# Layers' attention: V projected in full 128-token tiles and laid out by DMA, exps and normed output in single buffers

## The chip, the core and the metric

The kernel runs on one core of a Trainium2 chip. The metric is device time in microseconds, from the start of the program to its end; lower is better. TensorE is called PE below, VectorE DVE, ScalarE ACT, GpSimd POOL, and SyncE, which issues the DMAs, SP.

## What is computed

Sixteen sequences of 256 tokens with 128 channels go through four blocks, each followed by a layer norm. The change lies in the last block, six layers of local attention and a gated feed-forward. Of its reference this matters here:

```python
def attn_layer(x, Wqkv, qs, ksc, Wo):
    qkv = x @ Wqkv                       # x: 256 x 128, Wqkv: 128 x 3072
    q, k, v = split into 16 heads of 64
    q, k = l2norm(q) * qs, l2norm(k) * ksc, both rotated by position
    out = local_attention(q, k, v)       # windows of 32 queries
    return out @ Wo

def local_attention(q, k, v):            # w = 32, nw = 8 windows
    # window i sees the 64 keys and values of windows i-1 and i
    sim = einsum('bhwie,bhwje->bhwij', bq, bk2) * 8; masked
    attn = softmax(sim)
    return einsum('bhwij,bhwje->bhwie', attn, bv2)

for i in range(6):
    x = attn_layer(shift_tokens(x), ...) + x
    x = ffn_layer(shift_tokens(x), ...) + x
```

Everything is float32, except the mask, which is added to the scores as a bfloat16 matmul.

## The kernel before

`l1_network` holds the six layers. The order of work is written out by hand for each engine, in functions of the same name that run in the same order; semaphores join them (`after(engine, semaphore, value)` waits). A layer is a `prologue` (the first sequence's projections), then 16 times `attention(N, u, ...)`, in pairs u = 0, 1: the first pair stands alone, a loop makes passes for pairs 1 to 6, the last pair stands alone again. The feed-forward follows. `attention` has two half steps, j = 0 and 1, one for each 128 tokens of sequence N, and in both it also makes half of the projections of sequence N + 1 and finishes the output of the half before.

PE's order in a half step: wait for the turned weights (`weights_ready`), `masks`, `weigh` of the half before, two `project_qk` of the next sequence, two `project_v` of the next sequence, `scores`, `output`, two `turn_output`, `turn_weights`, then four `turn_qk` and two `project_qk` among each other. Four banks of PSUM, `pp`, are shared: q and k use banks 0 and 1, everything else alternates between 2 and 3, and a bank is taken again once the use before last has been read. The second `turn_output` of a half step so waits for DVE's `add_attention`.

V is needed with the 64 tokens of a window of keys (two windows of 32) on the partitions where the turned weights have them. PE multiplies 64 rows at a time (`weigh`), the weights and the values of the even and odd channel blocks (f = 0, 1) lying on partitions 0 to 63 and 64 to 127. A window with odd number takes its 64 values from `V`, one with even number from `Vx`, which is `V` shifted by 32 tokens. `project_v(N, m)` makes `V` for 64 tokens (m = 0 to 3) by two matmuls, one for each f, to the lower and the upper half of the partitions (L2061 to L2067); `copy_v` (ACT, L2311) copies the bank to `V[:, u, m, :]`, and once all four are there (`s_V`), SP makes `Vx` by four DMAs of whole rows (L1914 to L1918). `weights_ready` waits for both before the first half is weighed. u is the parity of the sequence: V and Vx have two buffers each.

The weights: DVE takes the maximum of the scores (`maxima`, L2450), subtracts it into `E`, ACT takes the exp in place (`exps`), DVE sums (`sum_exps`), PE turns them (`turn_weights`) and ACT copies them (`copy_weights`). After `weigh`, DVE scales into `On` (`norm_output`, L2470), PE turns it (`turn_output`) and ACT copies it. `E` and `On` have one buffer for each j. POOL adds the rotary products and normalises q and k.

Of the kernel before, what the change touches and what calls it, by code (L numbers as in the profile page):

```python
# [13 lines left out]
ACT = mybir.ActivationFunctionType  # L14
# [1659 lines left out]
def l1_network(nc, env, weights, consts):  # L1674
# [50 lines left out]
    with ExitStack() as ctx:  # L1725
# [37 lines left out]
        qkT = sb("qkT", [P, 2, I // P, T])  # L1763
        V = sb("V", [P, 2, 4, 512])
        Vx = sb("Vx", [P, 2, 4, 512])
        E = sb("E", [P, NT, 2, 512])
# [4 lines left out]
        On = sb("On", [P, NT, 2, 512])  # L1771
# [22 lines left out]
        s_vx = [sem(f"v_shifted{u}", False) for u in range(2)]  # L1794
# [83 lines left out]
        def _(sp):  # L1878
# [6 lines left out]
            with sp.Fori(0, LAYERS) as l:  # L1885
# [24 lines left out]
                with sp.Fori(0, NB // 2) as i:  # L1910
                    for u in range(2):

                        N = l * NB + 2 * i + u
                        after(sp, s_V, 4 * N + 4)  # L1914
                        for f in range(2):
                            lo, hi = 64 * f, 64 * f + W
                            sp.dma_start(Vx[lo:lo + W, u, 1:4, :], V[hi:hi + W, u, 0:3, :]).then_inc(s_vx[u], 16)
                            sp.dma_start(Vx[hi:hi + W, u, :, :], V[lo:lo + W, u, :, :]).then_inc(s_vx[u], 16)  # L1918
# [114 lines left out]
        def _(pe):  # L2033
# [27 lines left out]
            def project_v(N, m, bank):  # L2061
                after(pe, s_xT, N + 1)
                wv = wqkv[:, 2 * I:3 * I].rearrange("p (c f n) -> p f c n", c=4, f=2)
                for f in range(2):
                    last = nc.tensor.matmul(pp[64 * f:64 * f + 64, bank, :].rearrange("p (c n) -> p c n", c=4),  # L2065
                                            xT[:, 64 * m:64 * m + 64], wv[:, f, :, :], start=True, stop=True)
                last.then_inc(s_v, 1)  # L2067
# [9 lines left out]
            def turn_output(N, k, bank):  # L2077
                j, f = k // 2, k % 2
                after(pe, s_On, 4 * N + k + 1)
                for c in range(4):  # L2080
                    last = nc.tensor.transpose(pp[:, bank, c * P:(c + 1) * P], On[:, j, f, c * P:(c + 1) * P],  # L2081
# [33 lines left out]
            def turn_weights(N, j):  # L2115
                for e in range(2):
                    after(pe, s_On, 4 * N + 2 * j)
                    after(pe, s_E, 4 * N + 2 * j + e + 1)
                    for c in range(4):
                        last = nc.tensor.transpose(pW[:, e, c * P:(c + 1) * P], E[:, j, e, c * P:(c + 1) * P],  # L2120
# [18 lines left out]
            def weights_ready(pair, N, u, j):  # L2139
                after(pe, s_ET, 4 * N + 2 * j + 2)  # L2140
                if j == 0:
                    after(pe, s_V, 4 * N + 4)
                    pe.wait_ge(s_vx[u], 64 * (pair + 1))
# [151 lines left out]
        def _(act):  # L2295
# [15 lines left out]
            def copy_v(N, u, m, bank):  # L2311
                after(act, s_PV, 4 * (N - 1))
                after(act, s_v, 4 * N + m + 1)
                nc.scalar.copy(V[:, u, m, :], pp[:, bank, :]).then_inc(s_V, 1)
# [14 lines left out]
            def exps(N, j, e):  # L2329
                after(act, s_sub, 4 * N + 2 * j + e + 1)  # L2330
                nc.scalar.activation(E[:, j, e, :], E[:, j, e, :], ACT.Exp).then_inc(s_E, 1)  # L2331
# [394 lines left out]
```

## Time and profile before

| | us |
|---|---|
| median of 3 runs | 5327.94 (5325.83 to 5335.15) |
| profiled execution | 5325.95 |
| its span, first to last instruction | 5324.1 |
| mean granted TensorE clock | 0.933 of full |

| engine | busy us | share |
|---|---|---|
| PE matmul | 4457.0 | 84% |
| PE weight loads (beside the matmuls) | 3018.6 | 57% |
| DVE | 3369.7 | 63% |
| POOL | 2571.8 | 48% |
| ACT | 2441.2 | 46% |

The six layers take from about 1255 us to the end, the 96 sequences of attention most of that. A matmul of 512 columns in float32 shows as two records. In the timelines neighbouring records of one line are merged, so that a merged row's length runs to the modelled end of the last; the starts are exact. "issue" as the cause of an idle time means that the engine waited for nothing that the profile shows. Line numbers are those of the kernel before.

### The profile page before, as it was taken

Reading aid. Unit: us, or ns where it says so; the run is one execution under the profiler, and the core shown is the slowest. Engines: PE = TensorE matmul, PEld = TensorE weight load, DVE = VectorE, ACT = ScalarE, POOL = GpSimd, SP = SyncE. Lnnn points to the kernel's source line nnn. Section 1 sums busy time; section 2 is a strip of 40 time slices with the busy share of each in tenths; the row PEclk is TensorE's granted clock in tenths of the full one; section 3 lists DMA queues with packets and bytes.
Section 4 is the critical chain, followed back from the end, with each engine's and each line's share of the span. In section 5 each row is a group of like instructions: output and inputs, shape, how many; then the busy total and the mean of one; then the engine's idle time right before and its main releaser. Section 6 shows DMA issues by size and latency. Waiting matters only on the chain. (4 is left out here: it accounts for less than half of the span.)

```text
span 5324.1 us, 183366 instructions
## 1 busy us (share of the span) xinstructions
PE 4457.0 (84%) x70226; PEld 3018.6 (57%) x70227; DVE 3369.7 (63%) x7024; ACT 2441.2 (46%) x5161; POOL 2571.8 (48%) x4541
## 2 busy tenths in 40 slices
PE   8999938676888888888888888888888888888885
PEld 5777725563555555555555555555555556555563
DVE  3555532475766567766677666766667666676765
ACT  4555543133554435554355544544435554354542
POOL 0000000004776547775376753767537776377761
PEclk9999959797999999999999999999999999999997
DMA  1000003101111101111011110111101111011110
GB/s 37 4 4 4 1 0 80 30 0 54 31 30 24 39 20 31 30 24 39 20 31 24 30 40 20 31 24 30 40 20 25 29 30 33 20 31 30 30 23 32
DMA packets 76046, 143.02 MB, mean 27 GB/s; under 512 B 19654, under 2 KB 57748, under 8 KB 68116
## 3 DMA queue, kind: packets, MB, share of 16 engines
q1 hardware_dynamic: 75284, 131.92, 10.3%
q8 instruction: 593, 9.72, 0.8%
q14 instruction: 169, 1.38, 0.1%
HBM read 35.40 MB, written 4.19 MB: 7 GB/s over the span
## 5 line engine op out<-in xcount | busy, mean ns | idle before, releaser
L2439 DVE TENSOR_TENSOR n_tt<-n_pp,n_rot 128x1024 f32<-128x1024 f32 x768 | 925.3, 1222 | 650.8 <-ACT n_sq L2309 647.8
L1941 POOL TENSOR_TENSOR n_pre<-n_tt 128x512 f32<-128x512 f32 x768 | 965.6, 1276 | 481.5 <-DVE n_tt L2439 480.8
L2057 PE MATMUL n_pp<-n_wqkv,n_xT 128*128 128x512 f32 x1536 | 828.6, 643 | 10.6 <-ACT n_xT L2304 10.5
L2309 ACT ACTIVATE n_sq<-n_pp 128x512 f32<-128x512 f32 x768 | 458.9, 598 | 797.2 <-PE n_pp L2057 793.4
L1976 POOL TENSOR_TENSOR n_pre<-n_pre,n_rn 128x512 f32<-128x512 f32 x768 | 777.6, 1045 | 36.8 <-POOL n_rn L1964 36.8
L2446 DVE TENSOR_REDUCE n_ss<-n_sq 128x8 f32<-128x512 f32 x768 | 519.5, 676 | 0.0
L2331 ACT ACTIVATE n_E<-n_E 128x512 f32<-128x512 f32 x384 | 235.8, 630 | 595.6 <-DVE n_E L2458 595.6
L2074 PE MATMUL n_pp<-ident,n_pre 128*128 128x128 f32 x3072 | 416.0, 278 | 45.4 <-POOL n_pre L1976 41.8
L2074 PEld LDWEIGHTS n_pp<-ident,n_pre 128*128 128x128 f32 x3072 | 361.3, 144 | 161.5 <-issue 94.4
L2320 ACT COPY n_qkT<-n_pp 128x512 f32<-128x512 f32 x768 | 420.7, 604 | 54.3 <-PE n_pp L2074 52.8
L2088 PE MATMUL n_pp<-n_wo,n_OT 128*128 128x128 f32 x3072 | 406.4, 287 | 4.9 <-ACT n_OT L2326 4.9
L2476 DVE TENSOR_TENSOR n_On<-n_pW,n_ri 128x512 f32<-128x512 f32 x384 | 246.8, 685 | 225.9 <-PE n_pW L2133 224.9
L2088 PEld LDWEIGHTS n_pp<-n_wo,n_OT 128*128 128x128 f32 x3072 | 369.8, 197 | 23.6 <-ACT n_OT L2326 6.2
L2081 PE MATMUL n_pp<-ident,n_On 128*128 128x128 f32 x1536 | 241.8, 281 | 165.8 <-DVE X L2483 165.2
L2065 PE MATMUL n_pp<-n_wqkv,n_xT 128*64 128x512 f32 x1536 | 379.2, 612 | 0.0
L2133 PE MATMUL n_pW<-n_V,n_ET 64*32 64x64 f32 x12288 | 325.2, 237 | 39.9 <-issue 39.7
L2108 PEld LDWEIGHTS n_pS<-n_qkT 64*32 64x32 f32 x24576 | 254.2, 105 | 173.2 <-issue 173.2
L2057 PEld LDWEIGHTS n_pp<-n_wqkv,n_xT 128*128 128x128 f32 x1536 | 260.8, 201 | 158.0 <-issue 135.4
L2133 PE MATMUL n_pW<-n_Vx,n_ET 64*32 64x64 f32 x12288 | 309.4, 236 | 47.2 <-issue 41.4
L2453 DVE TENSOR_REDUCE n_nm<-n_pS 128x8 f32<-128x512 f32 x384 | 247.4, 686 | 139.8 <-PE n_pS L2108 139.8
L556 DVE CUSTOM_DVE_ANT_0 a_S<-a_pS,a_causal 128x128 f32<-128x128 f32 (+1 forms) x512 | 162.7, 356 | 264.9 <-PE a_pS L361 211.5
L296 POOL TENSOR_TENSOR a_rstd<-a_mv,neghalf 128x2 f32<-128x2 f32 x16 | 11.2, 701 | 653.1 <-DVE a_mv L124 653.1
(263 smaller groups left out, 8241.4 us busy)
## 6 DMA issues: line engine op xcount, KB each, us to landing
n_Vx<-n_V SPq DMA_DIRECT2D x192, 256.0 KB, 3.8
n_Vx<-n_V SPq DMA_DIRECT2D x192, 192.0 KB, 3.7
n_wqkv<-in_L_ffn_Wqkv SPq DMA_DIRECT2D x6, 1536.0 KB, 7.4
e_w<-in_L_ffn_w SPq DMA_DIRECT2D x32, 256.0 KB, 3.0
m_Y<-e_ye SPq DMA_DIRECT2D x64, 64.0 KB, 2.0
n_wo<-in_L_ffn_Wo SPq DMA_DIRECT2D x6, 512.0 KB, 7.2
a_xs<-in_L_attn_x SPq DMA_DIRECT2D x16, 128.0 KB, 2.1
x_kept<-X SPq DMA_DIRECT2D x1, 2048.0 KB, 8.5
```

The source lines that it names most:

```text
L1941: nc.gpsimd.tensor_tensor(d, s[0], s[1][:, :, ::-1, :], ALU.add).then_inc(s_add, 1)
L1976: nc.gpsimd.tensor_tensor(d, d, bcast(rn[:, j, t, 8 * half:8 * half + 8], 2, D), ALU.mult).then_inc(s_kn, 1)
L2057: nc.tensor.matmul(pp[:, c % 2, :], xT[:, j * P:(j + 1) * P], wqkv[:, t * I + 512 * half:t * I + 512 * half + 512], start=True, stop=True) ...
L2065: last = nc.tensor.matmul(pp[64 * f:64 * f + 64, bank, :].rearrange("p (c n) -> p c n", c=4), xT[:, 64 * m:64 * m + 64], wv[:, f, :, :], s ...
L2074: last = nc.tensor.transpose(pp[:, bank, g * P:(g + 1) * P], pre[:, j, t, o:o + P], ident[:, :])
L2088: last = nc.tensor.matmul(pp[:, bank, 0:C], OT[:, j, k % 2, k // 2, :], wo[:, k, :], start=(k == 0), stop=(k == I // P - 1))
L2108: last = nc.tensor.matmul(pS[W * w:W * w + W, e, i * 2 * W + o:(i + 1) * 2 * W], qkT[r:r + D, 0, i, q:q + W], qkT[r:r + D, 1, i, lo:q + W] ...
L2133: last = nc.tensor.matmul(pW[W * w:W * w + W, f, o:o + D], ET[r:r + D, e, c, W * w:W * w + W], v[r:r + D, u, m, o:o + D], start=True, stop ...
L2309: nc.scalar.activation(sq[:, c % 2, :], pp[:, c % 2, :], ACT.Square).then_inc(s_sq, 1)
L2320: nc.scalar.copy(qkT[:, t, 4 * half:4 * half + 4, j * P:(j + 1) * P], pp[:, bank, :].rearrange("p (g q) -> p g q", g=4)).then_inc(s_qkT, 1)
L2439: nc.vector.tensor_tensor(tt[:, c % 4, :, :].rearrange("p s (h d) -> p s h d", d=D), bcast(pp[:, c % 2, :].rearrange("p (h d) -> p h d", d ...
L2446: nc.vector.tensor_reduce(ss[:, j, t, 8 * half:8 * half + 8], sq[:, c % 2, :].rearrange("p (h d) -> p h d", d=D), AX.X, ALU.add).then_inc( ...
```

## The change

`project_v(N, m)` now makes one matmul of 128 tokens by 512 of V's 1024 channels (m counts half of the tokens and half of the channels). ACT copies it to a plain buffer `Vn` (token on the partition, two groups of 128 tokens, one buffer for all sequences). SP makes both layouts from it, 18 DMAs to a sequence instead of 4: after the first half's two copies ten, after the second's eight. Each of them takes 32 or 64 tokens and for each token four runs of 128 channels (512 bytes), which are side by side at the destination. `s_vx` counts all of them (18 x 16 = 288 a sequence). PE waits for `s_vx` alone before it weighs. ACT, before each copy to `Vn`, waits until the sequence before has been placed; it needs the pair's number for that. `E` and `On` lose their dimension j, and their writers wait for the reader of the half step before instead of that of the sequence before.

```diff
         nt = sb("nt", [P, 2 * H])
         pre = sb("pre", [P, NT, 2, I])
         qkT = sb("qkT", [P, 2, I // P, T])
+        Vn = sb("Vn", [P, NT, I])
         V = sb("V", [P, 2, 4, 512])
         Vx = sb("Vx", [P, 2, 4, 512])
-        E = sb("E", [P, NT, 2, 512])
+        E = sb("E", [P, 2, 512])
         ET = sb("ET", [P, 2, 4, P])
         nm = sb("nm", [P, NT, 2, 8])
         rs = sb("rs", [P, NT, 2, 8])
         ri = sb("ri", [P, NT, 2, 8])
-        On = sb("On", [P, NT, 2, 512])
+        On = sb("On", [P, 2, 512])
         OT = sb("OT", [P, NT, 2, 4, P])
...
-        s_vx = [sem(f"v_shifted{u}", False) for u in range(2)]
+        s_vx = [sem(f"v_placed{u}") for u in range(2)]
...
                         N = l * NB + 2 * i + u
-                        after(sp, s_V, 4 * N + 4)
-                        for f in range(2):
-                            lo, hi = 64 * f, 64 * f + W
-                            sp.dma_start(Vx[lo:lo + W, u, 1:4, :], V[hi:hi + W, u, 0:3, :]).then_inc(s_vx[u], 16)
-                            sp.dma_start(Vx[hi:hi + W, u, :, :], V[lo:lo + W, u, :, :]).then_inc(s_vx[u], 16)
+                        for j in range(NT):
+                            after(sp, s_V, 4 * N + 2 * j + 2)
+                            for f in range(2):
+                                lo, hi = 64 * f, 64 * f + W
+                                own = Vn[:, j, :].rearrange("p (c f n) -> p f c n", c=4, f=2)[:, f, :, :]
+
+                                def place_v(to, rows, m, src):
+                                    sp.dma_start(to[rows:rows + src.shape[0], u, m, :].rearrange(
+                                        "p (c n) -> p c n", c=4), src).then_inc(s_vx[u], 16)
+
+                                place_v(V, lo, 2 * j, own[0:64, :, :])
+                                place_v(V, lo, 2 * j + 1, own[64:P, :, :])
+                                place_v(Vx, hi, 2 * j, own[0:W, :, :])
+                                place_v(Vx, lo, 2 * j + 1, own[W:P - W, :, :])
+                                if j == 0:
+                                    place_v(Vx, lo, 2, own[P - W:P, :, :])
...
             def project_v(N, m, bank):
                 after(pe, s_xT, N + 1)
-                wv = wqkv[:, 2 * I:3 * I].rearrange("p (c f n) -> p f c n", c=4, f=2)
-                for f in range(2):
-                    last = nc.tensor.matmul(pp[64 * f:64 * f + 64, bank, :].rearrange("p (c n) -> p c n", c=4),
-                                            xT[:, 64 * m:64 * m + 64], wv[:, f, :, :], start=True, stop=True)
-                last.then_inc(s_v, 1)
+                j, half = m // 2, m % 2
+                nc.tensor.matmul(pp[:, bank, :], xT[:, j * P:(j + 1) * P],
+                                 wqkv[:, 2 * I + 512 * half:2 * I + 512 * half + 512],
+                                 start=True, stop=True).then_inc(s_v, 1)
...
             def weights_ready(pair, N, u, j):
                 after(pe, s_ET, 4 * N + 2 * j + 2)
                 if j == 0:
-                    after(pe, s_V, 4 * N + 4)
-                    pe.wait_ge(s_vx[u], 64 * (pair + 1))
+                    after(pe, s_vx[u], 288 * (pair + 1))
...
-            def copy_v(N, u, m, bank):
+            def copy_v(N, u, m, bank, pair):
                 after(act, s_PV, 4 * (N - 1))
+                after(act, s_vx[1 - u], 288 * (pair + u))
                 after(act, s_v, 4 * N + m + 1)
-                nc.scalar.copy(V[:, u, m, :], pp[:, bank, :]).then_inc(s_V, 1)
+                nc.scalar.copy(Vn[:, m // 2, 512 * (m % 2):512 * (m % 2) + 512], pp[:, bank, :]).then_inc(s_V, 1)
...
-                        copy_v(N + 1, 1 - u, 2 * j, bank("v", 2 * j, 1))
-                        copy_v(N + 1, 1 - u, 2 * j + 1, bank("v", 2 * j + 1, 1))
+                        copy_v(N + 1, 1 - u, 2 * j, bank("v", 2 * j, 1), pairs[0] + u)
+                        copy_v(N + 1, 1 - u, 2 * j + 1, bank("v", 2 * j + 1, 1), pairs[0] + u)
...
-            layers(act, attention, feed_forward, prologue)
+            pairs = [None]
+
+            def on_pair(i):
+                pairs[0] = i
+
+            layers(act, attention, feed_forward, prologue, on_pair=on_pair)
...
-                after(dve, s_ETp, 4 * (N - 1) + 2 * j + 2)
+                after(dve, s_ETp, 4 * N + 2 * j)
                 for e in range(2):
                     after(dve, s_max, 4 * N + 2 * j + e + 1)
-                    nc.vector.tensor_tensor(E[:, j, e, :].rearrange("p (i s) -> p i s", s=2 * W),
+                    nc.vector.tensor_tensor(E[:, e, :].rearrange("p (i s) -> p i s", s=2 * W),
...
             def norm_output(N, j):
                 after(dve, s_ri, 2 * N + j + 1)
-                after(dve, s_OTp, 4 * (N - 1) + 2 * j + 2)
+                after(dve, s_OTp, 4 * N + 2 * j)
                 after(dve, s_PV, 4 * N + 2 * j + 2)
                 r = ri[:, j, :, :].rearrange("p e (c f) -> p f c e", f=2)
                 for f in range(2):
-                    nc.vector.tensor_tensor(On[:, j, f, :].rearrange("p (c e d) -> p c e d", c=4, e=2),
+                    nc.vector.tensor_tensor(On[:, f, :].rearrange("p (c e d) -> p c e d", c=4, e=2),
```

The other lines of the diff only drop the index j of `E` and `On` where they are read (L2081, L2120, L2331, L2465).

## Rows read from the trace of the kernel before

**Rows 1.** The page: busy time of the engines; the group of V's projection.
```profile
PE 4457.0 (84%) x70226; PEld 3018.6 (57%) x70227; DVE 3369.7 (63%) x7024; ACT 2441.2 (46%) x5161; POOL 2571.8 (48%) x4541
...
L2065 PE MATMUL n_pp<-n_wqkv,n_xT 128*64 128x512 f32 x1536 | 379.2, 612 | 0.0
```

**Rows 2.** Busy time by stretch (PE, PEld, DVE, ACT, POOL; granted clock; DMA): two sequences.
```profile
1403.75:1443.13 39.38, 32.34 (x667) 21.07 (x655) 25.18 (x37) 18.18 (x34) 25.61 (x47) 0.91 0.12 27
1443.13:1475.53 32.40, 29.53 (x668) 20.01 (x655) 24.91 (x37) 18.18 (x34) 25.17 (x45) 1.00 0.14 31
```

**Rows 3.** Timeline (start, length, engine, line, tile, count, idle), PE, one undisturbed sequence.
```profile
1447.28 0.66 PE L2081 MATMUL n_pp<-ident,n_On 128*128 128x128 f32 x4 [0.97 <-DVE X L2483]
1447.77 1.04 PE L2120 MATMUL n_pW<-ident,n_E 128*128 128x128 f32 x8
...
1454.89 1.97 PE L2057 MATMUL n_pp<-n_wqkv,n_xT 128*128 128x512 f32 x4
1456.79 1.94 PE L2065 MATMUL n_pp<-n_wqkv,n_xT 128*64 128x512 f32 x8
1458.66 1.46 PE L2108 MATMUL n_pS<-n_qkT 64*32 64x32 f32 x128
```

**Rows 4.** Timeline, PE, narrow windows that split its records around that V projection.
```profile
1456.27 0.59 PE L2057 MATMUL n_pp<-n_wqkv,n_xT 128*128 128x512 f32 x1
...
1457.70 1.03 PE L2065 MATMUL n_pp<-n_wqkv,n_xT 128*64 128x512 f32 x4
...
1458.13 0.60 PE L2065 MATMUL n_pp<-n_wqkv,n_xT 128*64 128x512 f32 x2
```

**Rows 5.** Timeline, DVE, the same sequence.
```profile
1455.50 1.28 DVE L2476 TENSOR_TENSOR n_On<-n_pW,n_ri 128x512 f32<-128x512 f32 x2
...
1460.18 1.29 DVE L2453 TENSOR_REDUCE n_nm<-n_pS 128x8 f32<-128x512 f32 x2 [0.55 <-PE n_pS L2108]
```

**Rows 6.** Timeline, ACT, copies of V in three half steps.
```profile
1403.14 0.59 ACT L2314 COPY n_V<-n_pp 128x512 f32<-128x512 f32 x1 [0.27 <-PE n_pp L2065]
...
1442.52 0.59 ACT L2314 COPY n_V<-n_pp 128x512 f32<-128x512 f32 x1 [0.27 <-PE n_pp L2065]
...
1457.92 0.59 ACT L2314 COPY n_V<-n_pp 128x512 f32<-128x512 f32 x1 [0.42 <-PE n_pp L2065]
```

**Rows 7.** Timeline, PE, the prologue of layer 1.
```profile
1936.38 1.08 PE L2065 MATMUL n_pp<-n_wqkv,n_xT 128*64 128x512 f32 x4
...
1938.45 1.08 PE L2065 MATMUL n_pp<-n_wqkv,n_xT 128*64 128x512 f32 x4
```

**Rows 8.** DMA issues (KB each, us to landing), and line 1021 (ns min/median/max).
```profile
n_Vx<-n_V SPq DMA_DIRECT2D x192, 256.0 KB, 3.8
...
m_Y<-e_ye SPq DMA_DIRECT2D x64, 64.0 KB, 2.0
...
L1021 SPq DMA_DIRECT2D m_Y<-e_ye x64: 606/608/789, 863.5 to 966.7; - x64
```

**Rows 9.** Busy time by stretch: line 1021's transfers, then V's.
```profile
948.00:950.00 2.00, 2.00 (x8) 1.03 (x7) 0.00 (x0) 1.83 (x4) 0.00 (x0) 1.00 0.31 66
1407.00:1409.00 2.00, 1.10 (x10) 1.10 (x11) 2.00 (x5) 1.55 (x4) 2.00 (x3) 1.00 1.04 229
```

**Rows 10.** Timeline, ACT, layer 1, V's last copy in the prologue, the next one.
```profile
1943.70 0.59 ACT L2314 COPY n_V<-n_pp 128x512 f32<-128x512 f32 x1 [0.42 <-PE n_pp L2065]
...
1961.94 0.59 ACT L2314 COPY n_V<-n_pp 128x512 f32<-128x512 f32 x1 [0.42 <-PE n_pp L2065]
```

**Rows 11.** Timeline, PE, at the end of a pass of the loop.
```profile
1416.48 0.60 PE L2096 MATMUL n_pS<-n_win,n_eye 128*128 128x512 bf16 x2 [2.76 <-issue]
```

**Rows 12.** Busy time by stretch, the same place.
```profile
1413.75:1414.00 0.25, 0.00 (x0) 0.00 (x0) 0.00 (x0) 0.24 (x1) 0.25 (x1) 1.00 0.24 66
1416.20:1418.90 2.70, 1.80 (x77) 1.16 (x78) 0.01 (x1) 0.00 (x0) 2.06 (x6) 0.67 0.03 6
1417.25:1423.50 6.25, 5.00 (x132) 2.83 (x112) 1.50 (x3) 0.60 (x1) 3.48 (x15) 0.50 0.01 3
```

More of the change, by code:

```diff
@@ L2080, in turn_output @@
                 for c in range(4):
-                    last = nc.tensor.transpose(pp[:, bank, c * P:(c + 1) * P], On[:, j, f, c * P:(c + 1) * P],
+                    last = nc.tensor.transpose(pp[:, bank, c * P:(c + 1) * P], On[:, f, c * P:(c + 1) * P],
                                                ident[:, :])
@@ L2119, in turn_weights @@
                     for c in range(4):
-                        last = nc.tensor.transpose(pW[:, e, c * P:(c + 1) * P], E[:, j, e, c * P:(c + 1) * P],
+                        last = nc.tensor.transpose(pW[:, e, c * P:(c + 1) * P], E[:, e, c * P:(c + 1) * P],
                                                    ident[:, :])
@@ L2330, in exps @@
                 after(act, s_sub, 4 * N + 2 * j + e + 1)
-                nc.scalar.activation(E[:, j, e, :], E[:, j, e, :], ACT.Exp).then_inc(s_E, 1)
+                nc.scalar.activation(E[:, e, :], E[:, e, :], ACT.Exp).then_inc(s_E, 1)
             def copy_weights(N, j, e):
@@ L2345, in prologue @@
                     elif kind == "v":
-                        copy_v(N, 0, c, bank)
+                        copy_v(N, 0, c, bank, l * (NB // 2))
                     else:
@@ L2464, in sum_exps @@
                     after(dve, s_E, 4 * N + 2 * j + e + 1)
-                    nc.vector.tensor_reduce(rs[:, j, e, :], E[:, j, e, :].rearrange("p (i s) -> p i s", s=2 * W),
+                    nc.vector.tensor_reduce(rs[:, j, e, :], E[:, e, :].rearrange("p (i s) -> p i s", s=2 * W),
                                             AX.X, ALU.add).then_inc(s_rs, 1)
```

## The prediction

> **What bounds the kernel now.** I read four views in this order: the page's busy shares, the busy time of single sequences, the timelines of TensorE (PE) and VectorE (DVE) inside one sequence, and the DMA issues. By the page PE is busy 84% of the span, the next engine 63% [rows 1]. Inside one sequence of the layers PE is busy 29.53 of 32.40 us while DVE has 24.91 and GpSimd (POOL) 25.17 [rows 2], so in this stage PE's queue sets the pace. PE does not run free: once in each half step it waits 0.97 us for DVE's addition to X before turn_output [rows 3]. That wait is the end of a chain that begins with the last score matmul: DVE's maxima, subtractions, one sum of squares, the addition. But DVE itself was idle for 0.55 us before those maxima, waiting for the scores [rows 5]. So time that PE saves ahead of the scores moves the whole chain forward, up to 0.55 us in a half step; beyond that DVE is late.
>
> The second thing to see is the end of a pass of the loop over pairs of sequences. A sequence that holds it takes 39.38 us instead of 32.40 [rows 2]: PE idles 2.76 us with nothing to wait for but its own issue [rows 11], a short transfer of 66 GB/s x 0.25 us = 16 KB lies at its start, and from 1417.25 to 1423.50 the granted clock is 0.50, that is the level of 1.2 GHz, right after that idle time [rows 12]. The loop has six passes in each of six layers, so this happens 30 times: about 30 x 7 = 210 us of the span, which the change does not aim at but could disturb.
>
> **V's projection, PE.** Before, one project_v is two matmuls on 128x64 tiles, on the two column halves of the array. They run side by side: two project_v take 1458.66 - 1456.79 = 1.87 us with 8 records [rows 3], where eight one after the other at the 0.43 us between 1457.70 and 1458.13 [rows 4] would take 3.4. The full tile has one matmul (two records) with the same 512 columns, so the streaming time stays 2 x 0.43 = 0.86 us; halving the number of matmuls gains nothing by itself. What goes is the change of tile shape between the projections of q, k and of V. The last q/k record starts at 1456.27 [rows 4] and V starts at 1456.79 [rows 3], 0.52 instead of 0.43: 0.09 us. The first two V records take 1457.70 - 1456.79 = 0.91 instead of 0.86: 0.05 us. After the last V record (1458.13) [rows 4] the scores, again another shape, start at 1458.66 [rows 3], 0.53: this 0.10 stays, because 128x128 to 64x32 is a change too. Saving per half step 0.09 + 0.05 = 0.14 us; it lies on PE's path and is below DVE's 0.55. V is projected for the next sequence in 15 of 16 steps, two half steps each, six layers: 180 x 0.14 = 25.2 us. Bounds: 0 if the 0.14 belongs to something else than the shape, 180 x 0.24 = 43 us if the exit goes as well.
>
> In the prologue V and q/k alternate: from one V to the next 1938.45 - 1936.38 = 2.07 us [rows 7] instead of 1.72, but there DVE's rotation and sum follow closely and I grant only 0.3 us to a layer: 1.8 us (0 to 6 x 1.05 = 6.3).
>
> **The copies of V, ScalarE (ACT).** Still four of 0.59 us to a sequence [rows 6], now to Vn. New is the wait on the placement of the previous sequence's V ahead of each. Behind it on ACT stand the exps, the copies of the turned output and of the weights, and PE and DVE wait for all of these, so a late placement would cost in full.
>
> **The placement, SyncE (SP) and DMA.** Before: 4 DMAs, 2 x (192 + 256) = 896 KB, with the landing of the larger at 3.8 us [rows 8]. After: 18 DMAs, ten after the first half's copies (per f three of 128 KB and two of 64 KB, together 1024 KB) and eight after the second's (896 KB), in runs of 512 bytes. The nearest rows are those of line 1021, SBUF to SBUF, 64 KB in runs of 512 bytes: 608 ns to issue (606 to 789), 2.0 us to land [rows 8]. Its transfers moved 66 GB/s at a share of 0.31, so 213 GB/s at full share, V's large ones 229 at 1.04, so 220 [rows 9]: short runs cost little. At 213 GB/s the second burst takes 4.2 us and the first 4.8; the issues take 8 x 0.61 = 4.9 and 10 x 0.61 = 6.1 us. So the second placement is down 4.9 + 3.8 = 8.7 us after the copies (6.9 with the landing of 2.0). Its deadline: the copy that ends the second half ends at 1442.52 + 0.59 = 1443.11, and the next to Vn starts at 1457.92 [rows 6], 14.8 us later. Cover left: 6 us. It is gone from (14.8 - 3.8) / 8 = 1.38 us an issue on. The first burst hasn't to be down before that either, only to leave SP's queue free after 16 us. In each layer's prologue all 18 follow one another: the last copy ends at 1943.70 + 0.59 = 1944.29, the next is at 1961.94 [rows 10], and even with nothing issued before the last copy 18 x 0.61 + 3.8 = 14.8 us fit into 17.7. V is weighed more than half a step later still. Cost: nothing. SP does nothing else inside the layer; the feed-forward weights are issued ahead of the loop as before.
>
> Against this stands a rule of the Trainium skill, DMA: Bandwidth & Descriptors, section Bandwidth: small transfers are dominated by their descriptors, 64 KB taking 0.95 us at 138 GB/s. By that figure an estimate for the second burst is 896 KB / 138 GB/s = 6.5 us instead of 4.2; it would still be down before the deadline. This case's row for 64 KB, 213 GB/s at full share, speaks for more.
>
> **E and On in one buffer each.** maxima now waits for the turned weights of the half step before: PE did those at 1447.77 to 1448.81 [rows 3], and the next maxima start at 1460.18 [rows 5], 11 us later. norm_output waits for the half before's turned output, done at 1447.94 [rows 3], and starts at 1455.50 [rows 5]. Both are long satisfied and in both cases PE's own order guarantees it. Behind those waits on DVE stand rotations and maxima, but nothing is held. Cost nothing.
>
> **PE's program is shorter.** Each project_v loses two weight loads and two matmul records; one pass of the loop is 32 instructions shorter, and what stands ahead of the loop in a layer 48 or a few more. After the idle 2.76 us PE starts masks and weigh, does 77 matmuls and 78 loads, and stops again within 1416.20 to 1418.90 with 0.9 us idle in that window [rows 12]. I read this as the end of a block of code, with the next one still to be fetched. A head that lies 50 instructions earlier in its block has 50 more to do before the stop, at this rate (155 in about 1.3 us) up to 0.4 us at each of 30 places. I take 0.1: 3 us (bounds 0 to 12).
>
> **Sum.** 25.2 + 1.8 + 3 = 30 us. Profiled execution: 5325.95 us (span 5324.1), so 5296. The median of the three runs is 5327.94, 2 us above it: 5298.
>
> **Rivals.** *No gain.* The full tile streams as the pair did and the 0.14 us is not the shape's, or it comes back at the loop's end, whose slow stretch differs from pass to pass. For it: the column halves already overlap perfectly, and the first saving is a third of a microsecond in 32. Against it: the 0.09 and 0.05 are there, while records of one shape stand 0.43 apart. 5318 to 5338; chance 0.19.
>
> *The placement is late* (slower). If an issue of 256 runs costs not 0.61 but, say, 1.6 us, because the queue takes runs and not bytes, the second placement ends 8 x 1.6 + 3.8 = 16.6 us after the copies, 1.8 past the deadline, once for each of 90 sequences: 162 us, 5460. For it: there are 1792 runs where there were 64 long ones; against it: line 1021 shows 0.61 for 128 runs. It decides from 1.38 us an issue on. Chance 0.08.
>
> *The placement meets the loop's end* (slower). At 1403.14 + 0.59 = 1403.73 [rows 6] the last copy ends, at 1413.75 PE's code is fetched [rows 12]; if the DMA engines are then still busy, the two fetches that follow each other wait behind up to 2 us of queued transfers, 30 x 4 = 120 us, 5418. It takes a burst that lasts over 10.0 us; I have 6.9 to 8.7. Chance 0.06.
>
> *The loop's head crosses a block* (slower than forecast). The first stop after the idle time comes 77 + 78 = 155 records past the head [rows 12]. If moving the head by 50 instructions puts it at the very end of a block, PE does nearly nothing before the second fetch, and the 1.3 us of those records are lost 30 times: 39 us, so 5337 (with the 3 us above not gained, 5340). It decides if the head stands less than 50 instructions into its block now, which no row here shows. Chance 0.07. The Trainium skill, Runtime: NRT & Kernel Launch, section Instruction fetch mechanics, has the rule behind it: only sequential code is fetched ahead, in blocks of 16 KB or 256 instructions, and a taken branch out of the window fetches its target first. By that rule, the trace agrees (idle with the cause "issue", and 16 KB moved), and an estimate from its 256 puts the head some 85 to 100 into its block, 35 to 50 after the change, on the safe side.
>
> **Chances and range.** Forecast (5285 to 5316) 0.55; more than forecast, with the exit of the shape too or shorter slow stretches, 0.05 (down to 5268: 43 + 6.3 + 12 = 61 us). About 0.2% (11 us) is what this measurement can tell from no change. Faster 0.60, same 0.19, slower 0.21. The range takes in the lower bound and, above, the block rival: 5268 to 5345; it leaves out the two late-transfer rivals.
>
> **What would show it.** PE: from the first q/k projection to the scores 3.63 us instead of 3.77 (1454.89 to 1458.66), undisturbed sequences 32.1 instead of 32.4. DVE's idle before maxima down by 0.14. ACT's copies of V still wait for PE only, not for a DMA; issues near 0.6 us. Wrong it is if SP's issues pass 1.4 us, if ACT's copies wait for DMA, or if the idle at the loop's end grows beyond 2.8 us.

## The result and the profile after

| | before | after |
|---|---|---|
| median of 4 runs, us | 5329.66 (5325.83 to 5335.15) | 5242.58 (5238.51 to 5245.6) |
| ratio, 95% interval | | 0.9835 (0.9818 to 0.9852) |
| span of the profiled execution, us | 5324.1 | 5236.7 |

The change makes the kernel 87 us faster; I had forecast 30, and my range ended at 60. The page of the changed kernel, first PE and the other engines, then V's projection and the two groups of weigh (with the idle time ahead of their matmuls and its cause), then the DMAs of the placement:

```profile
PE 4403.9 (84%) x69459; PEld 3064.0 (59%) x69459; DVE 3355.6 (64%) x7024; ACT 2443.9 (47%) x5161; POOL 2569.8 (49%) x4541
...
L2076 PE MATMUL n_pp<-n_wqkv,n_xT 128*128 128x512 f32 x768 | 370.6, 603 | 0.0
...
L2144 PE MATMUL n_pW<-n_V,n_ET 64*32 64x64 f32 x12288 | 310.3, 238 | 24.8 <-issue 24.8
...
L2144 PE MATMUL n_pW<-n_Vx,n_ET 64*32 64x64 f32 x12288 | 309.5, 238 | 18.0 <-issue 12.5
...
n_V<-n_Vn SPq DMA_DIRECT2D x768, 128.0 KB, 2.6
n_Vx<-n_Vn SPq DMA_DIRECT2D x384, 128.0 KB, 2.5
n_Vx<-n_Vn SPq DMA_DIRECT2D x576, 64.0 KB, 2.2
```

V's projection keeps PE busy 370.6 us instead of 379.2 [rows 1] with half the records: as predicted, the two column halves had already run side by side. The same two groups of weigh in the kernel before:

```profile
L2133 PE MATMUL n_pW<-n_V,n_ET 64*32 64x64 f32 x12288 | 325.2, 237 | 39.9 <-issue 39.7
L2133 PE MATMUL n_pW<-n_Vx,n_ET 64*32 64x64 f32 x12288 | 309.4, 236 | 47.2 <-issue 41.4 <-ACT n_ET L2336 5.7
```

The two groups alternate within weigh. Their idle time with the cause "issue", added up, fell from 81.1 to 37.3 us. Weigh isn't touched by the change at all. I had not looked at it.

The saving of the half step that I did forecast is there. The timeline of PE in the changed kernel, and of DVE beside it:

```profile
1450.31 1.99 PE L2069 MATMUL n_pp<-n_wqkv,n_xT 128*128 128x512 f32 x4
1452.13 1.88 PE L2076 MATMUL n_pp<-n_wqkv,n_xT 128*128 128x512 f32 x4
1453.94 0.29 PE L2119 MATMUL n_pS<-n_qkT 64*32 64x32 f32 x9
```
```profile
1455.47 1.29 DVE L2469 TENSOR_REDUCE n_nm<-n_pS 128x8 f32<-128x512 f32 x2 [0.40 <-PE n_pS L2119]
```

From the first q/k projection to the scores 1453.94 - 1450.31 = 3.63 us, where [rows 3] have 3.77. DVE's idle time ahead of the maxima went from 0.55 [rows 5] to 0.40. So PE's saving did pass through to DVE.

For the whole account I took the starts of PE's records in each of the 30 passes of the loop over pairs (from one branch back to the next; two sequences) and formed the mean of every step. One pass takes 71.47 us before and 68.69 after, 2.78 less, and 30 x 2.78 = 83 of the 87 us lie there.

| step of a pass, start to start, us | before | after | less |
|---|---|---|---|
| first weigh, behind the branch | 3.24 | 2.74 | 0.50 |
| q/k projections right after it | 3.27 | 2.85 | 0.42 |
| second weigh | 2.27 | 1.41 | 0.86 |
| third weigh | 1.44 | 1.41 | 0.03 |
| fourth weigh | 2.08 | 1.41 | 0.67 |
| the other three pairs of q/k projections | 5.71 | 5.46 | 0.25 |
| V's four projection pairs | 7.58 | 7.39 | 0.19 |
| everything else | 45.88 | 46.02 | -0.14 |

A weigh is 128 weight loads and 128 matmuls, and runs through in 1.41 us if nothing stops it. Counted in instructions of PE from the branch, the stops of the kernel before inside weigh stand always at the same three places: 159, 927 and 2207. These are 159, 159 + 3 x 256 and 159 + 8 x 256, so PE's code comes in blocks of 256 instructions. The page lists the packets that carry it, 593 of 16 KB each:

```profile
q8 instruction: 593, 9.72, 0.8%
```

In the changed kernel the only stop inside weigh in a pass stands at 209. Around one stop of the kernel before, in the fourth weigh of a pass, busy time by stretch (stretch, length, then PE, PEld, DVE, ACT, POOL, granted clock, DMA share and GB/s):

```profile
1467.75:1468.00 0.25, 0.25 (x2) 0.08 (x1) 0.25 (x1) 0.25 (x2) 0.25 (x1) 1.00 0.30 66
1468.90:1469.90 1.00, 1.00 (x95) 0.96 (x95) 1.00 (x2) 0.25 (x1) 1.00 (x2) 1.00 0.00 0
1470.00:1470.50 0.50, 0.03 (x2) 0.00 (x0) 0.50 (x2) 0.00 (x0) 0.50 (x2) 1.00 0.00 0
1470.50:1471.00 0.50, 0.42 (x34) 0.34 (x33) 0.50 (x1) 0.00 (x0) 0.50 (x2) 1.00 0.00 0
```

Such a packet (0.25 us x 66 GB/s = 16 KB) begins to move just before 1468; PE goes through weigh at 95 loads and 95 matmuls a microsecond, stands still from 1470.0 and goes on at 1470.5, some 2.6 us after the packet. No other transfer is under way while it waits (DMA share 0.00), so it isn't contention. The fourth weigh of a pass in the changed kernel, in full:

```profile
1463.80:1464.05 0.25, 0.25 (x3) 0.00 (x0) 0.25 (x2) 0.18 (x1) 0.25 (x1) 1.00 0.34 72
1464.20:1465.60 1.40, 1.40 (x129) 1.31 (x128) 1.40 (x2) 0.27 (x1) 1.40 (x2) 1.00 0.00 0
```

Here a packet comes at 1463.8 too, but the block in use lasts longer than weigh does. Over the stops of all passes, in these two kernels and in the variants below, PE goes on 2.1 to 3.0 us after the start of the packet, 2.5 in the mean.

### The profile page after: what moved, and what is told of

Read it like the earlier page. It is cut to its first block and busy times, and to the rows that moved or that the text cites. A ratio compares the mean times of both kernels' runs of the same rounds, so it can differ in the third digit from the quotient of the medians.

```text
span 5236.7 us, 183609 instructions
## 1 busy us (share of the span) xinstructions
PE 4403.9 (84%) x69459; PEld 3064.0 (59%) x69459; DVE 3355.6 (64%) x7024; ACT 2443.9 (47%) x5161; POOL 2569.8 (49%) x4541
## 3 DMA queue, kind: packets, MB, share of 16 engines
q8 instruction: 593, 9.72, 0.8%
## 5 line engine op out<-in xcount | busy, mean ns | idle before, releaser
L2069 PE MATMUL n_pp<-n_wqkv,n_xT 128*128 128x512 f32 x1536 | 823.2, 639 | 10.4 <-ACT n_xT L2314 10.1
L2331 ACT COPY n_qkT<-n_pp 128x512 f32<-128x512 f32 x768 | 423.7, 603 | 68.3 <-PE n_pp L2085 66.1
L2076 PE MATMUL n_pp<-n_wqkv,n_xT 128*128 128x512 f32 x768 | 370.6, 603 | 0.0
L2144 PE MATMUL n_pW<-n_V,n_ET 64*32 64x64 f32 x12288 | 310.3, 238 | 24.8 <-issue 24.8
L2144 PEld LDWEIGHTS n_pW<-n_Vx,n_ET 64*32 64x32 f32 x12288 | 265.4, 111 | 109.8 <-issue 109.8
```

Source lines behind the costliest of these rows:

```text
L2069: nc.tensor.matmul(pp[:, c % 2, :], xT[:, j * P:(j + 1) * P], wqkv[:, t * I + 512 * half:t * I + 512 * half + 512], start=True, stop=True) ...
L2076: nc.tensor.matmul(pp[:, bank, :], xT[:, j * P:(j + 1) * P], wqkv[:, 2 * I + 512 * half:2 * I + 512 * half + 512], start=True, stop=True). ...
L2144: last = nc.tensor.matmul(pW[W * w:W * w + W, f, o:o + D], ET[r:r + D, e, c, W * w:W * w + W], v[r:r + D, u, m, o:o + D], start=True, stop ...
L2331: nc.scalar.copy(qkT[:, t, 4 * half:4 * half + 4, j * P:(j + 1) * P], pp[:, bank, :].rearrange("p (g q) -> p g q", g=4)).then_inc(s_qkT, 1)
```

## The experiments

There were two theories at first. **A, code blocks**: the shape of the tile brings what was forecast, and the other 55 to 60 us come from PE's program being shorter, so that its blocks end elsewhere. **B, data movement**: short runs in place of long rows, or the single buffers, freed something. All waits added below are for a semaphore that has long had its value.

**V in two tiles again.** In the changed kernel:

```diff
-                nc.tensor.matmul(pp[:, bank, :], xT[:, j * P:(j + 1) * P], wqkv[...512 columns...],
-                                 start=True, stop=True).then_inc(s_v, 1)
+                for e in range(2):
+                    o = j * P + 64 * e
+                    last = nc.tensor.matmul(pp[64 * e:64 * e + 64, bank, :], xT[:, o:o + 64],
+                                            wqkv[...the same 512...], start=True, stop=True)
+                last.then_inc(s_v, 1)
```

> The changed kernel with V projected in two 128x64 tiles again (two matmuls to a bank, 64 tokens each; the result and everything else as in the changed kernel). Theory A (code blocks): the change gains 25 to 33 us by one tile shape in a row and some 55 us because PE's program is shorter: the ends of its 256-instruction blocks, at instruction 159 of a loop pass before and at 209 after, no longer fall into weigh. This kernel has both undone, so about 5327 (5320 to 5335), with stops inside weigh again (before: 110 weigh phases with a gap, 81 us; after: 53, 37 us). Theory B (data movement): what went beyond 30 us comes from the placement DMAs in short runs in place of long rows, or from single buffers; then about 5272.

Measured: 5329.65 us, ratio to before 1.0007 (0.9995 to 1.0019). All of the gain is gone, with the 18 DMAs, `Vn` and the single buffers still in place. Theory B falls: together the placement and the single buffers bring and cost nothing beyond the interval, 0.12% or 6 us. The block ends are back at 161 of a pass, and so is the idle time in weigh:

```profile
L2147 PE MATMUL n_pW<-n_V,n_ET 64*32 64x64 f32 x12288 | 322.1, 234 | 55.9 <-issue 55.9
L2147 PE MATMUL n_pW<-n_Vx,n_ET 64*32 64x64 f32 x12288 | 306.7, 233 | 35.3 <-issue 29.6 <-ACT n_ET L2350 5.7
```

**Two buffers for E and On again**, PE's count unchanged:

```diff
-        E = sb("E", [P, 2, 512])
+        E = sb("E", [P, NT, 2, 512])
-                after(dve, s_ETp, 4 * N + 2 * j)
+                after(dve, s_ETp, 4 * (N - 1) + 2 * j + 2)
```

(and the same for `On` and `s_OTp`.)

> The changed kernel with E and On in two buffers each again and their old waits; PE's instruction count is unchanged. Theory A: within 0.1% of the changed kernel, 5238 to 5248. Theory B, if the single buffers bring something: slower, up to 5300.

Measured: 5235.63 us, ratio 0.9836 (0.9801 to 0.9871) beside the changed kernel's 0.9835. Nothing, as expected.

**The full tile with waits in place of the saved instructions.** In `project_v` of the changed kernel, k = 4 and then k = 8:

```diff
+                for _ in range(k):
+                    pe.wait_ge(s_clear, 3)
                 nc.tensor.matmul(pp[:, bank, :], xT[:, j * P:(j + 1) * P],
```

> The changed kernel, with four extra instructions on PE ahead of each full-tile projection of V (waits for a semaphore that has long had its value), so that its instruction count is that of two tiles. Theory A: the blocks end again where they ended before the change, the shape's gain of 25 to 33 us stays, the rest is lost: about 5298 (5290 to 5306). Theory B: the count doesn't matter, 5243 to 5250 (the waits themselves are hidden under matmuls).

> The changed kernel with eight waits ahead of each full-tile projection of V. The trace of the run with four showed that two waits stand in one instruction, so that four waits had restored only half of the count (first block end of a pass at instruction 185); eight restore all of it, with the block end at 161 as in the kernel with two tiles. Code blocks: the shape's 25 to 33 us stay and the rest goes, 5290 to 5306, with the stops near instructions 929 and 2209 of a pass back. If the length of PE's code doesn't matter: 5240 to 5255 as with four waits.

Measured: 5247.67 us (0.9847, 0.9818 to 0.9877) with four and 5312.9 (0.9979, 0.9970 to 0.9989) with eight. With four the expectation of theory A failed: the trace counts 2 instructions more for each projection, not 4, since two waits go into one instruction, and the first block end was at 185. With eight it is at 161 as with two tiles, the stops at 929 and 2209 are back, and a gain of only 0.2% is left of the 1.65%. Beside the run with two tiles at the same place (1.0007) this is the shape's share: 0.28%, 15 us, with some 8 us of uncertainty either way by the two intervals, less than the 25 I expected. Inside the passes a pair of q/k projections takes 1.82 us and one of V's 1.81, against 1.91 and 1.87 with two tiles, at the same block ends: that is the 0.14.

**The kernel before, only moved.** n waits once, at the start of PE's program for the layers, where it idles for 20 us anyway:

```diff
             pe.wait_ge(s_clear, 3)
             pe.wait_ge(s_cast, 2)
+            for _ in range(n):
+                pe.wait_ge(s_clear, 3)
```

The idle time hides only the first of them. With 206 waits the first matmul of the layers comes 1 us late. With 300 and more PE isn't ready in time: an instruction that holds two of the waits takes 0.106 us, and the first matmul comes later by 7 us with 300 waits, 10 with 362 to 372, 12 with 414, 14 with 432 and 17 with 492 (each counted from the `x_kept` DMA ahead of the layers). The first row is the kernel before, the second the one with 362 waits:

```profile
1257.90 0.69 PE L2050 MATMUL n_pp<-ident,n_xs 128*128 128x128 f32 x2 [21.32 <-DMA n_qks<-in_L_ffn_k_scale]
...
1264.39 0.68 PE L2050 MATMUL n_pp<-ident,n_xs 128*128 128x128 f32 x2 [30.94 <-issue]
```

The first branch of the layers is later by nearly the same amount, so every moved kernel below carries these microseconds once, as a cost of the padding and not of its place. The times are given as measured.

With n = 206:

> The kernel before, with 206 such waits once, at the start of PE's program for the layers, where PE idles anyway; the first block inside a pass then ends at instruction 209 instead of 159, and all later ones move with it. Nothing else is touched. Theory A: 30 to 60 us faster than before (5270 to 5300), without the stops at instructions 927 and 2207 of a pass. Theory B: 5330.

Measured: 5383.18 us, ratio 1.0105 (1.0080 to 1.0130). The move was half of what I meant, since two waits go into one instruction, and put the block end at 57 of a pass instead of 209. That a change without any work in it costs 1.05%, some 56 us, speaks for theory A even so, but it wasn't what I had expected. With n = 414:

> The kernel before with 414 waits (207 instructions) once at the start of PE's program for the layers. The first try with 206 waits moved the first block end of a pass to instruction 57 and cost 56 us; this one should put it at 208, where the changed kernel has it. Code blocks: 30 to 60 us faster than before, 5265 to 5300, stops at 927 and 2207 gone. If the first try was slower for the waits themselves: slower again, by twice as much.

Measured: 5277.31 us, ratio 0.9906 (0.9889 to 0.9923), with the block end at 208. So 0.9% of the 1.65% can be had without the change, and 1.2% if the 12 us of the waits at the start are left out. Its weigh groups:

```profile
L2133 PE MATMUL n_pW<-n_V,n_ET 64*32 64x64 f32 x12288 | 308.0, 233 | 53.9 <-issue 53.7
L2133 PE MATMUL n_pW<-n_Vx,n_ET 64*32 64x64 f32 x12288 | 306.6, 233 | 5.7 <-ACT n_ET L2338 5.7
```

53.7 us of idle time are left: the pass is 34 instructions longer than the changed one, so that with the same block end at its start another one falls at 2256 into the fourth weigh, where a stop of 0.8 us stands.

**The changed kernel, only moved**, by 432 and 372 waits:

> The changed kernel with 432 waits (some 215 instructions) once at the start, so that a pass begins near the start of a block: first block end at about instruction 250. Code blocks: the stop inside the first weigh of a pass (0.8 us a pass) goes, as all of weigh lies in the block fetched for the branch; if no other block end falls badly, 10 to 40 us faster than the changed kernel, 5200 to 5232. If the place of the blocks doesn't matter: 5241.

> The changed kernel with 372 waits (some 185 instructions) once at the start: first block end at about instruction 24 of a pass, so that the branch fetches a block of which only 24 instructions are left. Code blocks: the idle time at the head of the first weigh grows by about the 1.3 us of work that now lies behind the second fetch, 30 times 39 us, and less or more by where the other ends fall: 5265 to 5310. If the place doesn't matter: 5241.

Measured: 5258.11 us (0.9869, 0.9844 to 0.9893) and 5352.06 us (1.0056, 1.0035 to 1.0078). The first of the two missed: the block end at 1530 falls 197 instructions into the third weigh and makes a new stop of 0.78 us, more than is won at the head (0.15 us in the first weigh and 0.28 in the projections behind it), and 14 us are the waits at the start.

The second is slower than the kernel before. It has the rival of the block crossing in it, but that is only a part of its 110 us over the changed kernel. Of the 90 us by which its 30 passes are longer, the first weigh takes 1.10 us a pass, 33 us: this is the crossing, to be set against my 39, and the projections right behind it get 0.40 us a pass back. Another 27 us (0.91 a pass) stand in the third weigh, where a block end falls 226 instructions in. And the stop at the branch itself is longer, by 33 us. The row of `masks`, first in the changed kernel, then here:

```profile
L2107 PE MATMUL n_pS<-n_win,n_eye 128*128 128x512 bf16 x384 | 124.3, 408 | 93.3 <-issue 87.1 <-ACT n_qkT L2331 5.6
...
L2107 PE MATMUL n_pS<-n_win,n_eye 128*128 128x512 bf16 x384 | 126.9, 415 | 126.8 <-issue 120.6 <-ACT n_qkT L2333 5.6
```

The DMA records show why. A block ends 68 instructions ahead of the branch, so that the block behind the loop is being fetched when the branch is taken, and the packet of the branch's target starts 0.6 us behind that one. The page counts 624 code packets here instead of 593. The kernel before with its block end at 57 has the same in all 30 passes (69 instructions ahead of the branch, 624 packets), and so have 6 of the 30 passes of the changed kernel at 60 below. Where two packets overlap, PE goes on 4.7 to 4.8 us after the branch, and 3.5 to 3.7 in all other passes.

**A rule, tried blind.** Behind the head of a pass, in all kernels so far, a block end stopped a weigh (by 0.6 to 1.0 us) from its instruction 189 on, and not at 156 or earlier. The four weighs of a pass begin at 8, 678, 1350 and 2018 in the kernel before and at 8, 669, 1333 and 1992 in the changed one.

> A rule read from the seven kernels so far, tried blind: PE stops inside a weigh (256 instructions) for 0.7 to 0.9 us where a block of 256 ends behind its instruction 189 or later, and doesn't where the end is at 156 or earlier. The kernel before, with 362 waits (some 180 instructions) once at the start, puts the block ends of a pass at 235, 747, 1515 and 2027, so at 227, 69, 165 and 9 of the four weighs. By the rule only the head's stop is left, the one at 2256 of the run moved to 208 is gone (0.8 us x 30 = 24 us): 5248 to 5262. The rule being wrong: 5277 or more.

> The changed kernel with 300 waits (some 149 instructions) once at the start: block ends at 60, 828, 1340 and 2108, that is 52, 159, 7 and 116 of the four weighs. By the rule no stop behind the head; at the head 52 instead of 201 instructions of weigh before the second fetch, so 0.9 to 1.0 us more there (1.6 to 1.7 us as in the run moved to 57): 30 times 27 to 30 us more than the changed kernel, 5265 to 5275. If the head doesn't matter: 5241.

> The changed kernel with 492 waits once at the start: block ends at 220, 732, 1500 and 2012, that is 212, 63, 167 and 20 of the four weighs. By the rule (no stop at 156 or earlier, a stop from 189 on) 167 is in the open stretch. No stop there: the changed kernel's time or a little less for the shorter stop at the head, 5232 to 5243. A stop: about 5255.

Measured: the kernel before with its block ends at 235 takes 5233.51 us, ratio 0.9828 (0.9802 to 0.9854), as fast as the changed kernel, although its first matmul of the layers comes 10 us late. A gain of the whole size can be had without the change. The stops of weigh behind the head are gone in all three, as the rule has it; 167 instructions into a weigh is no stop either. Weigh's idle time in the first of them:

```profile
L2133 PE MATMUL n_pW<-n_V,n_ET 64*32 64x64 f32 x12288 | 302.4, 234 | 0.0
L2133 PE MATMUL n_pW<-n_Vx,n_ET 64*32 64x64 f32 x12288 | 298.7, 234 | 32.0 <-issue 25.9 <-ACT n_ET L2338 5.7
```

The sizes were off: 5233 where I expected 5248 to 5262, and 5305.71 (0.9949, 0.9933 to 0.9965) for the changed kernel at 60 where I expected 5265 to 5275. At 60 the stop at the head is 1.75 us instead of 0.82, 28 us in 30 passes, as expected. Of the rest 7 us are the waits at the start and 9 us are more idle time at the branch (the 6 passes with two packets), and the q/k projections run 20 us longer, with more time at the lower clock. The same 3807 us from the start of the layers on in each (columns as above), first the kernel before at 235, then the changed one at 60:

```profile
1257.00:5064.00 3807.00, 3297.72 (x63443) 2190.09 (x63444) 2662.17 (x4207) 1883.14 (x3456) 2479.13 (x4387) 0.96 0.12 29
```
```profile
1257.00:5064.00 3807.00, 3248.71 (x60942) 2221.59 (x60943) 2601.39 (x4117) 1840.54 (x3372) 2419.93 (x4269) 0.94 0.23 55
```

The clock is 0.96 on average in the one and 0.94 in the other, and 63443 matmuls are done instead of 60942. (The greater DMA share of the second is the placement.)

From 1257 us to the end the granted clock stood at its level of 1.2 GHz for 333 us in the first, 517 us in the second, 439 in the kernel before and 433 in the changed one. Of that, 126, 239, 201 and 184 us lie in the 30 passes. The stop at the head is as long at 235 as in the changed kernel, so it alone doesn't set the slow time. What does is not shown. The changed kernel at 220 took 5250.73 us (0.9861, 0.9839 to 0.9882), just above what I expected without a stop, and 17 us of that are the waits at the start: its passes are as long as the changed kernel's own (68.59 and 68.69 us).

**The shape at the good place.** The changed kernel with eight waits in `project_v` and 366 at the start, against the kernel before at 235:

> The changed kernel with both: eight waits ahead of each projection of V, so that a pass has the instruction count of two tiles, and 366 waits once at the start, so that the block ends stand at 235, 747, 1515 and 2027 as in the kernel before moved to 235. Against that run only the tile's shape differs (placement and single buffers have cost nothing). 180 half steps x 0.14 = 25 us for the shape, or the 17 us by which the runs with full and with two tiles at 161 differ: 5206 to 5218. If the shape's saving is covered by something else: 5233.

Measured: 5247.86 us, ratio 0.9861 (0.9841 to 0.9881), not faster than 0.9828. Both carry the same 10 us at the start. In its passes each pair of q/k and of V projections is shorter, 1.82 and 1.81 us instead of 1.91 and 1.87, 0.15 together, as forecast. But the block with the last projections and scores of a pass is now run through so fast that the next one isn't there: the last `scores` takes 1.93 us instead of 1.43, and the pass 68.60 instead of 68.69. What the shape saves, the fetch takes back. Outside the passes the profiled execution is 13 us slower, with 272 us at the lower clock there against 207. Why is not shown; what else differs between the two, the placement and the single buffers, cost nothing at 161, and no run measures it at 235. So the shape's 0.14 us are real and local, and what they bring to the end depends on the block ends again: 15 us at 161, nothing at 235.

**The placement's cover.** Each placement DMA is followed by one or two of the same source to spare DRAM, counted by the same semaphore (the values that are waited for grow with it):

```diff
                                     sp.dma_start(to[...], src).then_inc(s_vx[u], 16)
+                                    for _ in range(k):
+                                        sp.dma_start(env["spare"][u, next(spare), ...], src).then_inc(s_vx[u], 16)
```

> The changed kernel with each placement DMA followed by another of the same source to spare memory, both counted by the semaphore that ACT and PE wait for: 36 DMAs a sequence. In the changed kernel the last copy of a sequence ends 13.8 us before the next copy into Vn starts; 16 issues of 0.65 us and 2.6 us of landing are 13.0 us, so it should just be hidden: within 0.3% of the changed kernel, 5235 to 5260. If the placement already binds (the rival), every sequence gets about 5 us longer: 5700.

> The same with two spare DMAs behind each: 54 a sequence. SP needs 54 x 0.65 = 35 us where a sequence takes 31.4, and Vn isn't free before all have landed: 35 + 2.6 + two copies of V, 38.6 us a sequence instead of 31.4 (60 of them) and 37.2 (30, at the end of a pass): 5600 to 5800, with ACT's copies of V waiting for a DMA.

Measured: 5323.96 us (0.9991, 0.9976 to 1.0006) and 6170.44 us (one run). Neither is as expected: at twice the DMAs the cover I had put at 0.8 us isn't there. The last issue of a sequence ends 12.3 us after the last copy (median), where I had counted 10.4. The waits of ACT (us, times, longest), in the run with twice and in that with three times as many:

```profile
ACT n_Vn L2329 <- DMA spare<-n_Vn: 60.4, 32, 7.8
```
```profile
ACT n_Vn L2329 <- DMA spare<-n_Vn: 942.2, 90, 18.2
```

With twice the DMAs 32 of the 90 copies that could wait do so, 60 us together; this kernel is 81 us slower than the changed one. With three times as many all 90 wait, 10.5 us each. The changed kernel itself has no such row: its copies wait for PE alone, 109.5 us in 384 times. So the deadline that I gave exists, and the changed kernel stands clear of it by less than a factor of two in DMAs, if those to DRAM are like its own.

## Why the prediction was wrong

The direction is right, and so is the saving of the half step. The size is wrong because the sum held one term, the shorter program of PE, at 3 us, and it is some 70.

*V's projection*: 3.63 us instead of 3.77, as forecast to the hundredth, in three of four half steps of a pass. As a term of the sum, 25.2 us, it is 15 us at the end by the pair of runs at 161 and nothing by the pair at 235. In the prologues, from the first of V's projections to the scores, 0.7 us a layer are saved, 4 us where the sum has 1.8. *Copies, placement, single buffers*: nothing, by the run with two tiles (1.0007). The last issue ends 6.1 us after the last copy (median) and the next copy starts 9.3 us after that (8.0 at least), so that with 2.5 us of landing the second placement is down after 8.6 us and some 6 us of cover are left, as predicted. (The 64 long runs that I set against 1792 are 128: four DMAs of 32 partitions.) An issue takes 617 and 637 ns in the median where I took 608, the landing 2.2 to 2.6 us; the source line of the placement:

```profile
L1922 SPq DMA_DIRECT2D n_Vx<-n_Vn x960: 630/637/2101, 1269.1 to 5062.2; - x192
L1922 SPq DMA_DIRECT2D n_V<-n_Vn x768: 596/617/1902, 1267.6 to 5060.9; - x192
```

*PE's program is shorter*: this is the term that failed. I gave it 3 us, with 12 as the bound. I had seen that the head of the loop would move by 50 instructions within its block (159 to 209, exactly so) and that this matters to the first weigh. I asked about it at the head alone. The same 50 instructions move the ends of all blocks of a pass, and two of them stood inside the second and the fourth weigh: 0.86 + 0.67 = 1.53 us a pass, 46 us in 30 passes. At the head it is 0.50 and, behind it, 0.42 us, 28 us instead of 3. The second fetch comes at a fixed time after the first, so 50 instructions more are done ahead of it. That the q/k projections behind the head get shorter fits with more of them lying outside the stretch at half clock, but no run separates this. The rows were there: weigh with the cause "issue" for 81 us stood in the page, and 29.53 busy of 32.40 us left 2.87 us, of which I had named two times 0.97 only. The sequence that I took for undisturbed holds the stop at 1470. From the masks of the second weigh to those of the fourth, a sequence's length without the head, it is 31.40 us instead of 32.53, where I had forecast 32.1 instead of 32.4.

*The rivals.* No gain: wrong. The clock's part in it isn't where the gain comes from (433 us at the lower clock against 439). Late placement and its meeting the loop's end: neither in the changed kernel; the first begins at twice the DMAs. The crossing of a block: the mechanism is right, the side wasn't. The changed place is a good one, and at 24 the crossing costs 33 us in the first weigh, near the 39 that I gave it; the run is 110 us slower because that place has another stop in weigh and two packets at the branch, which I hadn't thought of.

Between the kernel before at 208 (0.9906) and at 235 (0.9828) a pass gets 1.58 us shorter. 0.84 of this is the stop in the fourth weigh. 0.36 lies in the first weigh and 0.44 in the projections behind it, and how much of these two is idle time and how much the clock can't be told apart from these runs, since both move together.

## What to carry to other kernels

Where an engine is idle with the cause "issue" inside a run of many short instructions, count its instructions from the last branch: stops at one fixed index, a multiple of 256 apart, were code fetches here, and adding or taking away instructions anywhere ahead moved them. A change of such a kernel should be measured at two or three places of its code before its gain is put down to what it does: here a kernel with nothing but waits added ran from 1.7% faster to 1% slower. The padding itself must be priced too: waits beyond what the idle time hides cost 10 to 17 us here. A block end shortly ahead of a branch back is a bad place as well (1.1 us a pass here). And matmuls that run side by side on the array's two column halves gained nothing here from one full tile but the change of shape, 0.14 us a half step.

## What the runs showed of the hardware

PE's code is fetched in packets of 16 KB (593 packets, 9.72 MB), 256 instructions (the distance of the stops), one block ahead. In most blocks the packet for the next one began to move 0.7 to 1.2 us after PE had entered the block, in some earlier or later, and at the stops PE went on 2.1 to 3.0 us after the packet's start, 2.5 in the mean. 256 instructions of weigh take 1.41 us, so a block that holds little else (a block end from instruction 189 of a weigh on) is through before the next is there. After a branch back, the fetch of the target's block stops PE for 2.76 us [rows 11], and the next block comes 3.1 us after that (1416.4 to 1419.5), with 23 or with 249 instructions left in the first alike (3.1 to 3.3 us in the means of all places). Where the block behind the loop was being fetched at the branch, PE stood 1.1 us longer. Two waits of PE in a row stand in one instruction (206 moved the code by 103) and take 0.106 us together when they are long satisfied. Neighbouring matmuls of different tile shapes cost 0.09 us at the end of the one and 0.05 to 0.10 at the start of the other (1.91 against 1.82 us and 1.87 against 1.81 in the runs with two and with full tiles at 161; the 0.10 by [rows 4]).
